# Two batches of a selective-scan layer as one unrolled pipeline over 64 heads

## The chip, the core and the metric

The kernel runs on one core of a Trainium2 chip. Five engines work beside each other and meet by semaphores: PE (TensorE, matmuls), DVE (VectorE), ACT (ScalarE), POOL (GpSimd) and SP (SyncE), which here only issues DMAs. The metric is the device time in microseconds, the median of several executions. Lower is better.

## The reference, cut to what matters

Two layers follow each other, each an attention-like part and a feed-forward part. The change touches the first part of layer 0 alone, a selective scan over 512 tokens, 2 batches and 32 heads of 128 channels:

```python
proj = x @ in_proj_w.T
gate, hbc, dt = jnp.split(proj, [I, I + CD], axis=-1)
conv = causal depthwise convolution of hbc, 4 taps
hbc = jax.nn.silu(conv + conv_b)
hs, B, C = jnp.split(hbc, [I, I + G * N], axis=-1)   # G = 8 groups, N = 128
B = jnp.tile(B, (1, 1, H // G, 1)); C = jnp.tile(C, (1, 1, H // G, 1))   # head h uses group h % 8
...
Y_diag = jnp.einsum('bclhn,bcshn,bhcls,bcshd->bclhd', Cc, Bc, Lmat, Xc)
Y_off = jnp.einsum('bclhn,bchdn,bhcl->bclhd', Cc, states_prev, state_decay)
y = (Y_diag + Y_off).reshape(b, s, H, P) + D_res
h32 = y * jax.nn.silu(gate)
g = h32.reshape(b, s, I // gs, gs)                   # gs = 512: four heads share one root
h32 = (g * jax.lax.rsqrt(var + EPS)).reshape(b, s, I)
return norm_w * h32 @ out_proj_w.T
```

## The kernel before

**Groups.** For each batch, B and C of eight groups are made first: 12 bf16 matmuls (`group_rows`, L450), ACT's first tap (L873), six taps on DVE (L1281), two tanh (L883), DVE's products `BT` and `CT` (L1288, L1291), four fp32 matmuls C x B and four transposes (L479, L482), two copies to `CB` and `Btok` (L887, L889) and POOL's mask (L1859). All eight stay in SBUF while the batch's heads run.

**Scan.** `scan_slot` on each engine writes one slot: head n is at stage 0, head n-1 at stage 1, head n-2 at stage 2. `slots` writes 8 slots, a hardware loop of three rounds of 8, and 7 more to drain; then batch 1 starts with its groups. PE in a slot: projection of `x` into bank 0 (`px`, L450), turning `xT` of head n-1 (L506), states of head n-2 into bank 5 (L515), the broadcast of `cs` of head n (the running sum of the decay) into bank 3 from three bf16 pieces `csT` (L527), a tile of the output product (L589, four heads' rows, into bank 6 or 7), the diagonal product of head n-1 into bank 5 (L538), once in four slots the sums of squares (L570), the chunk products into bank 4 (L551), the projection of the gate into bank 1 (`pg`, L450).

DVE in a slot: `Mm` (L1319), `gs` (L1325), tap 1 (L1333), `yv` (L1364, it empties bank 5), taps 2 and 3, three states (L1348, L1351) with the sum of an output tile (L1396) among them, and `xT` (L1381). One slot in four has ten of the root's twelve small steps (`root_step`, L1410 to L1426, 128x4) between these. ACT: tanh of the gate (L905), first tap (L910), `Xdt` (L919), exp `Em` (L927), the high half of the next weights `whl` (L932), `rel` (L937), square (L949), exp into bank 3 (L954), tanh into bank 2 (L959). POOL: `Xw` (L1812), `yb` (L1824), the low half of the weights (L1830), `CE` (L1835), the norm's factor on `wB` (L1841), the sum of squares (L1850).

Every engine works in the order written. The waits that set the pace: PE's turn waits for `xT`; PE's diagonal product waits for `Mm`, `Xdt` and for `yv` of the head before (`yc_done`), since both heads use bank 5; `yb` waits for `yv`, the square for `yb`, and the exp and the tanh that `xT` needs stand behind the square on ACT. In batch 1 the groups wait until batch 0 has left the buffers that they share with it. SP loads weights of 256 KB (`wA`) and 128 KB (`wB`) a head.

## Time and profile before

| | us |
|---|---|
| median of 3 runs | 1213.24 (1211.51 to 1215.61) |
| the profiled execution | 1214.29 |
| its span, first to last instruction | 1212.5 |
| PE busy | 958.9 (79%) |
| DVE busy | 899.9 (74%) |
| ACT busy | 657.0 (54%) |
| POOL busy | 520.6 (43%) |

The profile is of one execution; times in its rows are from the span's start. PE's matmuls overlap, so the distance between starts says more than one's duration. The granted clock is the share of full speed (2.4 GHz) that PE was given. A row of the timeline joins equal instructions that follow each other: start, duration of all, engine, line, operation, tiles, count, and in brackets the idle time before and who ended it.

### The profile page before, as it was taken

What the parts mean: (1) busy time and instruction counts of PE and PEld (TensorE: products, weight loads), DVE (VectorE), ACT (ScalarE), POOL (GpSimd) and SP (SyncE); (2) the same over time, 40 slices, a digit from 0 to 9 for tenths busy, and PEclk for the clock granted to TensorE, in tenths of its full rate; (3) what the DMA queues carried; (4) which work ended last, traced back from release to release, by engine and by line L of the source; (5) the groups of instructions that cost most, each with busy time, mean ns of one, the idle gap of its engine ahead of it and who ended that gap; (6) DMA issues with size and microseconds to landing.
All of it is one profiled execution on the core that took longest, in us unless ns stands there. A gap on an engine that the chain in (4) does not pass through costs nothing. (4 is left out here: it accounts for less than half of the span.)

```text
span 1212.5 us, 19613 instructions
## 1 busy us (share of the span) xinstructions
PE 958.9 (79%) x5524; PEld 645.3 (53%) x5524; DVE 899.9 (74%) x1667; ACT 657.0 (54%) x1421; POOL 520.6 (43%) x497
## 2 busy tenths in 40 slices
...
DMA packets 25353, 43.24 MB, mean 36 GB/s; under 512 B 3218, under 2 KB 15250, under 8 KB 24466
## 3 DMA queue, kind: packets, MB, share of 16 engines
...
HBM read 40.60 MB, written 1.05 MB: 34 GB/s over the span
## 5 line engine op out<-in xcount | busy, mean ns | idle before, releaser
L450 PE MATMUL bank<-hTs,whl 128*128 128x512 bf16 x768 | 177.7, 380 | 3.7 <-DVE u L1333 3.7
L1333 DVE SCALAR_TENSOR_TENSOR u<-bank,chn,u 128x511 f32<-128x511 f32 (+2 forms) x192 | 143.0, 745 | 29.2 <-ACT u L910 23.3
L589 PE MATMUL bank<-wB,yb 128*128 128x256 f32 x512 | 137.8, 418 | 3.9 <-DVE acc L1396 2.7
L1812 POOL TENSOR_TENSOR xbuf<-xbuf,dec 128x384 f32<-128x384 f32 x64 | 53.2, 832 | 172.6 <-ACT xbuf L919 172.6
L589 PEld LDWEIGHTS bank<-wB,yb 128*128 128x128 f32 x512 | 108.8, 214 | 22.8 <-DVE rg L1426 3.4
L450 PEld LDWEIGHTS bank<-hTs,whl 128*128 128x128 bf16 x768 | 75.4, 98 | 81.2 <-POOL whl L1830 6.4
L1878 POOL TENSOR_TENSOR hfs<-hf,hfs 128x512 bf16<-128x512 f32 x44 | 50.8, 1156 | 119.9 <-ACT hfs L1030 119.9
L450 PE MATMUL bank<-hTs,w13s 128*128 128x512 bf16 x372 | 94.7, 403 | 3.5 <-DVE hf L1536 1.9
L919 ACT ACTIVATE xbuf<-bank,dtv 128x128 f32<-128x128 f32 x256 | 72.5, 370 | 33.7 <-PE bank L506 33.7
L1824 POOL TENSOR_TENSOR yb<-yv,gs 128x512 f32<-128x512 f32 x64 | 81.3, 1271 | 6.7 <-DVE yv L1364 6.6
L1868 POOL TENSOR_TENSOR w13s<-w,w13s 128x256 bf16<-128x256 f32 (+1 forms) x22 | 23.2, 1090 | 135.4 <-ACT w13s L994 135.4
L753 PE MATMUL bank<-Ex,VW 128*80 128x512 f32 x128 | 72.8, 658 | 10.8 <-ACT Ex L1111 10.0
L538 PE MATMUL bank<-Mm,xbuf 128*128 128x128 f32 x512 | 68.8, 277 | 10.9 <-DVE yv L1364 8.9
L1103 ACT ACTIVATE aw<-bank,scl 128x512 f32<-128x512 f32 x64 | 43.4, 684 | 62.7 <-PE bank L740 37.1
L910 ACT ACTIVATE u<-bank,chn 128x512 f32<-128x512 f32 x64 | 49.7, 777 | 50.9 <-PE bank L450 50.9
L538 PEld LDWEIGHTS bank<-Mm,xbuf 128*128 128x128 f32 x512 | 66.1, 193 | 19.0 <-ACT xbuf L919 14.4
L1830 POOL TENSOR_TENSOR whl<-wA,whl 128x512 bf16<-128x512 f32 x64 | 74.2, 1160 | 2.0 <-ACT whl L932 1.9
L659 PE MATMUL bank<-w2s,hfs 128*128 128x256 bf16 x528 | 68.8, 283 | 7.9 <-POOL hfs L1878 7.9
L937 ACT ACTIVATE rel<-bank,cs 128x128 f32<-128x128 f32 x256 | 74.6, 406 | 0.0
L1281 DVE SCALAR_TENSOR_TENSOR gs<-bank,bcp,gs 128x511 f32<-128x511 f32 (+2 forms) x96 | 64.3, 739 | 6.0 <-ACT gs L873 5.9
L506 PE MATMUL bank<-cst,xT 128*128 128x128 f32 x256 | 41.0, 283 | 34.8 <-DVE xT L1381 34.8
L1348 DVE COPY xbuf<-bank 128x128 f32<-128x128 f32 x64 | 18.5, 288 | 67.1 <-PE bank L551 67.1
...
## 6 DMA issues: line engine op xcount, KB each, us to landing
wA<-in_win SPq DMA_DIRECT2D x65, 256.0 KB, 2.6
...
```

The source lines that it names most:

```text
L450: last = nc.tensor.matmul(out, wpart(a, kt), hpart(c, kt), start=n == 0, stop=n == 5)
L538: nc.tensor.matmul(bank[5][:, c * P:(c + 1) * P], Xdt[:, j % 2, c * P:(c + 1) * P], Mm[:, j % 2, c * P:(c + 1) * P], start=c == 0, stop=c ...
L589: last = nc.tensor.matmul(bank[6 + t % 2][:, 0:D], yb[:, y0 + m, t * P:(t + 1) * P], wB[:, y0 + m, :], start=m == 0, stop=m == HG - 1)
L659: last = nc.tensor.matmul(bank[6 + t // 2][:, (t % 2) * D:(t % 2 + 1) * D], hfs[:, a, m % 3, t * P:(t + 1) * P], w2s[:, c, f, :], start=Fa ...
L753: nc.tensor.matmul(bank[VB[par]][0:OC, :], VW[:, par, i * OC:(i + 1) * OC], Ex[:, i, :], start=i == 0, stop=i == 3).then_inc(q["a_PV"], 1)
L919: last = nc.scalar.activation(Xdt[:, j % 2, t * P:(t + 1) * P], bank[2][:, t * P:(t + 1) * P], ACT.Copy, scale=dtv[:, b * TB + t, bass.ds( ...
L937: last = nc.scalar.activation(rel[:, t * P:(t + 1) * P], bank[3][:, t * P:(t + 1) * P], ACT.Relu, scale=-1.0, bias=cs[:, b * TB + t, bass. ...
L1281: nc.vector.scalar_tensor_tensor(out=o, in0=bank[GB[par] + m][:, 0:S - d], scalar=w(m, 3 - d), in1=o, op0=ALU.mult, op1=ALU.add)\
L1333: nc.vector.scalar_tensor_tensor(out=u[:, i % 2, d:S], in0=bank[0][:, 0:S - d], scalar=chn[:, bass.ds(hcol, 1), 3 - d:4 - d].squeeze(1), i ...
L1812: nc.gpsimd.tensor_tensor(Xw[:, j % 2, :].rearrange("p (t n) -> p t n", n=P), Xdt[:, j % 2, 0:S - P].rearrange("p (t n) -> p t n", n=P), d ...
L1824: nc.gpsimd.tensor_tensor(yb[:, j, :], yv[:, j % 2, :], gs[:, j % 4, :], ALU.mult)\
L1830: nc.gpsimd.tensor_tensor(whl[:, nx, 1, :], wA[:, nx, :], whl[:, nx, 0, :], ALU.subtract).then_inc(q["wsplit"], 1)
```

## The change

One pipeline runs over all 64 heads, written out without a loop: 70 slots. The heads of a batch come in another order (`ORDER`): the 16 heads of groups 0 to 3 first, then the 16 of groups 4 to 7. Groups are numbered 0 to 15 over both batches. The first four are made ahead of the scan as before. The other 12 are made in slots 0 to 47, a quarter in each slot, all through bank 7: r0 (slot number divisible by 4) projects B and takes its taps, r1 makes `BT` and projects C with its taps, r2 turns `BT` and makes `CT`, r3 makes the product C x B. The output tiles have bank 6 alone. The sums of squares stand right behind the projection of `x`, and the root runs in that slot (r2), its last three steps behind `xT`; the sum of the tile stands behind `xT`, then follows the group's work.

The broadcast of `cs` comes from memory: once written to DRAM (`csd`), it is loaded for each head into all partitions (`csb`, 256 KB). The high half of the weights isn't copied: PE reads the upper 16 bits of each fp32 weight in place (`wAh`), and `wA` has four buffers. `wB` is loaded for four heads at once.

```diff
+N = B * H
+FIRST = 4
+ORDER = [HG * k + m for k in list(range(0, NG, 2)) + list(range(1, NG, 2)) for m in range(HG)]
...
-        wA = sb("wA", [P, 2, 512])
-        whl = sb("whl", [P, 2, 2, 512], bf16)
-        wB = sb("wB", [P, 8, D])
+        ug = sb("ug", [P, 2, S])
+        wA = sb("wA", [P, 4, 512])
+        wAh = wA[:, :, :].bitcast(bf16).rearrange("p a (n c) -> p a n c", c=2)[:, :, :, 1]
+        wAl = sb("wAl", [P, 2, 512], bf16)
+        wB = sb("wB", [P, 2, HG, D])
...
+        def head(n):
+
+            return (n, n // H, ORDER[n % H]) if 0 <= n < N else None
+
+        def out_tile(s):
+
+            m = s - 6
+            return (m % TB, m // TB) if 0 <= m < N else None
+
+        def former(gq):
+
+            b, g = gq // G, gq % G
+            return H * (b - 1) + ORDER.index(H - G + g) + 1 if b else 0
...
+                if h0 := head(s):
+                    n, b, hid = h0
+                    if n > 1:
+                        sp.wait_ge(q["rel_done"], n - 1)
+                    sp.dma_start(csb[:, n % 2, :], csd[b, hid].partition_broadcast(P)).then_inc(d_cb[n % 2], 16)
+                    if n > 3:
+                        sp.wait_ge(q["pg"], n - 3)
+                    sp.dma_start(wA[:, n % 4, :], io["win"][hid]).then_inc(d_wA[n % 4], 16)
...
+            def group_slot(s):
+
+                gq, r = FIRST + s // 4, s % 4
+                if gq >= B * G:
+                    return
+                if r == 0:
+                    pe.wait_ge(q["c_evac"], 2 * gq)
+                    if s == 0:
+                        pe.wait_ge(q["csr_done"], 1)
+                    group_half(gq, 0, bank[7][:, :]).then_inc(q["c_proj"], 1)
+                if r == 1:
+                    pe.wait_ge(q["c_step"], 6 * gq + 3)
+                    group_half(gq, 1, bank[7][:, :]).then_inc(q["c_proj"], 1)
+                if r == 2:
+                    pe.wait_ge(q["c_step"], 6 * gq + 6)
+                    pe.wait_ge(q["c_bc"], 2 * gq + 1)
+                    turn_keys(bank[7])
+                if r == 3:
+                    pe.wait_ge(q["c_evac"], 2 * gq + 1)
+                    pe.wait_ge(q["c_bc"], 2 * gq + 2)
+                    meet(gq, bank[7])
...
+                if e and e[0] == 0:
+                    k = e[1]
+                    if s - 1 < N:
+                        pe.wait_ge(q["rc_step"], 3 * (s - 1))
+                    pe.wait_ge(q["sq_add"], 3 * (k + 1))
...
+                    if TB * k + t:
+                        pe.wait_ge(q["oa_done"], TB * k + t)
+                    for m in range(HG):
+                        last = nc.tensor.matmul(bank[6][:, 0:D], yb[:, HG * (k % 2) + m, t * P:(t + 1) * P],
+                                                wB[:, k % 2, m, :], start=m == 0, stop=m == HG - 1)
...
+            def group_slot(s):
+
+                gq, r = FIRST + s // 4, s % 4
+                if gq >= B * G:
+                    return
+                if r == 0:
+                    act.wait_ge(q["c_bc"], 2 * gq - 3)
+                    act.wait_ge(q["c_proj"], 2 * gq + 1)
+                    group_taps(gq, 0, bank[7][:, :])
+                if r == 1:
+                    act.wait_ge(q["c_step"], 6 * gq + 3)
+                    group_tanh(gq, 0)
+                    act.wait_ge(q["c_bc"], 2 * gq - 2)
+                    act.wait_ge(q["c_proj"], 2 * gq + 2)
+                    group_taps(gq, 1, bank[7][:, :])
+                if r == 2:
+                    act.wait_ge(q["c_step"], 6 * gq + 6)
+                    group_tanh(gq, 1)
+                    keep_keys(gq, bank[7][:, :])
+                if r == 3:
+                    keep_meet(gq, bank[7][:, :])
...
+                nc.vector.scalar_tensor_tensor(out=BT[:], in0=thx[:, 0, :], scalar=1.0, in1=ub(gq, 0),
+                                               op0=ALU.add, op1=ALU.mult).then_inc(q["c_bc"], 1)
...
+            def group_slot(s):
+
+                gq, r = FIRST + s // 4, s % 4
+                if gq >= B * G or r == 3:
+                    return
+                if r == 1:
+                    keys(gq)
+                if r == 2:
+                    queries(gq)
+                    return
+                dve.wait_ge(q["c_raw"], 2 * gq + r + 1)
+                for d in (1, 2, 3):
+                    if d > 1:
+                        dve.wait_ge(q["c_step"], 6 * gq + 3 * r + d - 1)
+                    group_tap(gq, r, d, bank[7])
...
+                root(7, 8)
...
+                root(9, 10, 11)
...
+                group_slot(s)
...
+            for gq in range(FIRST):
+                first_group(gq)
+            clamp_gates(0)
+            for s in range(N + 6):
+                scan_slot(s)
```

The products, taps, roots and sizes are the same otherwise, and so is everything behind the scan.

**DVE, from `xT` of a head to `yv` of the next slot.** Before, in the loop:

```order
L1381 SCALAR_TENSOR_TENSOR xT<-bank,u 128x512
L1302 REGISTER_ALU
L1319 TENSOR_TENSOR Mm<-CB,bank 128x512
L1325 SCALAR_TENSOR_TENSOR gs<-thg,bank 128x512
L1332 REGISTER_ALU
L1333 ISA
L1333 SCALAR_TENSOR_TENSOR u<-bank,chn,u 128x511
L1364 ISA
L1364 SCALAR_TENSOR_TENSOR yv<-xT,chn,bank 128x512
```

After, in the first r1 slot that has an output tile (`ug` is the group's tile of taps, `L1401` makes `xT`, `L1382` `yv`):

```order
L1401 SCALAR_TENSOR_TENSOR xT<-bank,u 128x512
L1412 SCALAR_TENSOR_TENSOR acc<-bank,rg,acc 128x256
L1281 SCALAR_TENSOR_TENSOR BT<-thx,ug 128x512
L1273 SCALAR_TENSOR_TENSOR ug<-bank,bcp,ug 128x511
L1273 SCALAR_TENSOR_TENSOR ug<-bank,bcp,ug 128x510
L1273 SCALAR_TENSOR_TENSOR ug<-bank,bcp,ug 128x509
L1341 TENSOR_TENSOR Mm<-CB,bank 128x512
L1345 SCALAR_TENSOR_TENSOR gs<-thg,bank 128x512
L1424 TENSOR_SCALAR ssv<-bank 128x4
L1354 SCALAR_TENSOR_TENSOR u<-bank,chn,u 128x511
L1427 TENSOR_SCALAR nwt<-ssv 128x4
L1382 SCALAR_TENSOR_TENSOR yv<-xT,chn,bank 128x512
```

Between `xT` and `Mm` four instructions of the group now stand, and two steps of the root ahead of `yv`.

**PE, from the diagonal product to the turning of `xT`, in the slot with the sums.** Before:

```order
L589 MATMUL bank<-wB,yb 128x256 x4
L538 MATMUL bank<-Mm,xbuf 128x128 x4
L568 REGISTER_ALU
L570 MATMUL bank<-cst,sqa 128x1 x4
L551 MATMUL bank<-xbuf,Btok 128x128 x3
L450 MATMUL bank<-hTs,whl 128x512 x6
L496 REGISTER_ALU
L492 REGISTER_ALU
L450 MATMUL bank<-hTs,whl 128x512 x6
```

After, at the end of an r1 slot (`L563` the diagonal product, `L572` the chunk products, `L520` the sums):

```order
L563 MATMUL bank<-Mm,xbuf 128x128 x4
L572 MATMUL bank<-xbuf,Btok 128x128 x3
L438 MATMUL bank<-hTs,wbs 128x512 x6
L438 MATMUL bank<-hTs,wA 128x512 x4
L438 MATMUL bank<-hTs,wAl 128x512 x2
L438 MATMUL bank<-hTs,wA 128x512 x4
L438 MATMUL bank<-hTs,wAl 128x512 x2
L520 MATMUL bank<-cst,sqa 128x1 x4
L531 MATMUL bank<-cst,xT 128x128 x4
```

The sums moved from ahead of the chunk products to behind the next head's projection, and half a group's projection (`wbs`) stands ahead of the gate's.

## Rows read from the trace of the kernel before

**Rows 1.** Timeline: `xT` of five heads, and the step behind the scan.

```profile
107.13 0.69 DVE L1381 SCALAR_TENSOR_TENSOR xT<-bank,u 128x512 f32<-128x512 f32 x1 [0.77 <-ACT bank L959]
...
167.13 0.68 DVE L1381 SCALAR_TENSOR_TENSOR xT<-bank,u 128x512 f32<-128x512 f32 x1
...
360.65 0.69 DVE L1381 SCALAR_TENSOR_TENSOR xT<-bank,u 128x512 f32<-128x512 f32 x1
...
441.92 0.69 DVE L1381 SCALAR_TENSOR_TENSOR xT<-bank,u 128x512 f32<-128x512 f32 x1 [0.83 <-ACT bank L959]
...
697.37 0.69 DVE L1381 SCALAR_TENSOR_TENSOR xT<-bank,u 128x512 f32<-128x512 f32 x1
...
720.10 2.49 DVE L1446 TENSOR_TENSOR acc<-acc,gm 128x1024 f32<-128x1024 f32 x2
```

**Rows 2.** Timeline: taps of groups 3 and 7, three taps of one head.

```profile
70.55 4.02 DVE L1281 SCALAR_TENSOR_TENSOR gs<-bank,bcp,gs 128x511 f32<-128x511 f32 x6
...
92.32 4.02 DVE L1281 SCALAR_TENSOR_TENSOR gs<-bank,bcp,gs 128x511 f32<-128x511 f32 x6
...
104.05 2.31 DVE L1333 SCALAR_TENSOR_TENSOR u<-bank,chn,u 128x511 f32<-128x511 f32 x3 [5.84 <-ACT u L910]
```

**Rows 3.** Timeline: PE in one plain slot.

```profile
202.07 0.60 PE L506 MATMUL bank<-cst,xT 128*128 128x128 f32 x4
...
203.17 0.38 PE L527 MATMUL bank<-csT,identb 96*128 96x512 bf16 x1
...
203.39 1.89 PE L589 MATMUL bank<-wB,yb 128*128 128x256 f32 x8
...
205.12 1.05 PE L538 MATMUL bank<-Mm,xbuf 128*128 128x128 f32 x8
...
206.68 2.75 PE L450 MATMUL bank<-hTs,whl 128*128 128x512 bf16 x12
...
209.27 0.65 PE L506 MATMUL bank<-cst,xT 128*128 128x128 f32 x4
```

**Rows 4.** Timeline: DVE and ACT around the same slot.

```profile
201.10 0.68 DVE L1381 SCALAR_TENSOR_TENSOR xT<-bank,u 128x512 f32<-128x512 f32 x1
...
204.09 0.74 DVE L1364 SCALAR_TENSOR_TENSOR yv<-xT,chn,bank 128x512 f32<-128x512 f32 x1
...
207.74 0.58 ACT L959 ACTIVATE bank<-u 128x512 f32<-128x512 f32 x1
...
208.51 0.69 DVE L1381 SCALAR_TENSOR_TENSOR xT<-bank,u 128x512 f32<-128x512 f32 x1
```

**Rows 5.** Timeline: slot with the root, and PE in the next.

```profile
219.51 0.74 DVE L1364 SCALAR_TENSOR_TENSOR yv<-xT,chn,bank 128x512 f32<-128x512 f32 x1
...
223.00 1.00 POOL L1835 TENSOR_TENSOR xbuf<-CT,Em 128x384 f32<-128x384 f32 x1
...
223.10 0.92 DVE L1423 SCALAR_TENSOR_TENSOR nwt<-nwt,ssv 128x4 f32<-128x4 f32 x1
...
226.34 0.69 DVE L1381 SCALAR_TENSOR_TENSOR xT<-bank,u 128x512 f32<-128x512 f32 x1
...
227.16 0.65 PE L506 MATMUL bank<-cst,xT 128*128 128x128 f32 x4 [2.38 <-DVE xT L1381]
...
228.57 3.54 PE L589 MATMUL bank<-wB,yb 128*128 128x256 f32 x8
```

**Rows 6.** The page: weight loads, and the load of weights with us to landing.

```profile
L450 PEld LDWEIGHTS bank<-hTs,whl 128*128 128x128 bf16 x768 | 75.4, 98 | 81.2 <-POOL whl L1830 6.4
...
L538 PEld LDWEIGHTS bank<-Mm,xbuf 128*128 128x128 f32 x512 | 66.1, 193 | 19.0 <-ACT xbuf L919 14.4
...
wA<-in_win SPq DMA_DIRECT2D x65, 256.0 KB, 2.6
```

**Rows 7.** Windows: stretch, length, busy PE PEld DVE ACT POOL, granted clock, DMA share, GB/s.

```profile
101.00:360.00 259.00, 235.65 (x1420) 175.86 (x1418) 211.00 (x417) 189.54 (x476) 174.52 (x178) 0.96 0.17 49
227.70:232.70 5.00, 5.00 (x24) 4.21 (x23) 3.63 (x6) 4.26 (x13) 3.35 (x4) 0.66 0.00 0
```

More of the change, by code:

```diff
@@ L88, in build_block @@
         etot = sb("etot", [P, NT, H])
-        csp = sb("csp", [P, NT, PIECES, H], bf16)
-        csT = sb("csT", [PIECES * H, T], bf16)
+        csb = sb("csb", [P, 2, S])
+        csd = nc.dram_tensor("csd", (B, H, S), fp32, kind="Internal").ap()
         wbs = sb("wbs", [P, 2, G, 512], bf16)
@@ L473, in group_products @@
-            def group_products(g, b):
-                pe.wait_ge(q["c_bc"], 2 * (G * b + g) + 2)
-                if not (type(g) is int and G * b + g == 0):
-                    pe.wait_ge(q["c_evac"], G * b + g)
-                for t in range(TB):
-                    last = nc.tensor.matmul(bank[2][:, t * P:(t + 1) * P], BT[:, t * P:(t + 1) * P],
-                                            CT[:, bass.ds(g, 1), t * P:(t + 1) * P].squeeze(1), start=True, stop=True)
-                for t in range(TB):
-                    last = nc.tensor.transpose(bank[3][:, t * P:(t + 1) * P], BT[:, t * P:(t + 1) * P], ident)
-                last.then_inc(q["c_mm"], 1)
@@ new lines, in turn_keys, with meet @@
+            def turn_keys(out):
+                for t in range(TB):
+                    last = nc.tensor.transpose(out[:, t * P:(t + 1) * P], BT[:, t * P:(t + 1) * P], ident)
+                last.then_inc(q["c_mm"], 1)
+            def meet(gq, out):
+                for t in range(TB):
+                    last = nc.tensor.matmul(out[:, t * P:(t + 1) * P], BT[:, t * P:(t + 1) * P],
+                                            CT[:, gq % G, t * P:(t + 1) * P], start=True, stop=True)
+                last.then_inc(q["c_mm"], 1)
@@ L531, in scan_slot @@
-                out_slot(i, it, b)
-                if h1:
-                    j = h1[0]
-                    pe.wait_ge(q["xdt_done"], n1 + 1)
-                    pe.wait_ge(q["M_done"], n1 + 1)
-                    since("yc_done", n1)
-                    for c in range(TB):
-                        nc.tensor.matmul(bank[5][:, c * P:(c + 1) * P], Xdt[:, j % 2, c * P:(c + 1) * P],
-                                         Mm[:, j % 2, c * P:(c + 1) * P], start=c == 0, stop=c == 0,
-                                         skip_group_check=True)
@@ L542, in scan_slot @@
-                if h1:
-                    since("rc_step", 3 * n1)
-                if (e := out_event(i, it, 7)) and e[0] == 0:
-                    pe.wait_ge(q["rg_step"], ROOT * (NG * b + e[2]) + 1)
-                sums_slot(i, it, b)
-                if h1:
-                    j = h1[0]
-                    pe.wait_ge(q["xw_done"], n1 + 1)
-                    for c in range(TB - 1):
-                        last = nc.tensor.matmul(bank[4][:, c * P:(c + 1) * P], Btok[:, j, c, :],
-                                                Xw[:, j % 2, c * P:(c + 1) * P], start=True, stop=True)
-                    last.then_inc(q["ps"], 1)
@@ new lines, in scan_slot @@
+                if h1:
+                    n = h1[0]
+                    pe.wait_ge(q["xdt_done"], n + 1)
+                    pe.wait_ge(q["M_done"], n + 1)
+                    if n:
+                        pe.wait_ge(q["yc_done"], n)
+                    else:
+                        pe.wait_ge(q["c_step"], 6 * FIRST)
+                    for c in range(TB):
+                        nc.tensor.matmul(bank[5][:, c * P:(c + 1) * P], Xdt[:, n % 2, c * P:(c + 1) * P],
+                                         Mm[:, n % 2, c * P:(c + 1) * P], start=c == 0, stop=c == 0,
+                                         skip_group_check=True)
+                    if n:
+                        pe.wait_ge(q["rc_step"], 3 * n)
+                    if e and e[0] == 0:
+                        pe.wait_ge(q["rg_step"], ROOT * e[1] + 1)
+                    pe.wait_ge(q["xw_done"], n + 1)
+                    for c in range(TB - 1):
+                        last = nc.tensor.matmul(bank[4][:, c * P:(c + 1) * P], Btok[:, h1[2] % G, c, :],
+                                                Xw[:, n % 2, c * P:(c + 1) * P], start=True, stop=True)
+                    last.then_inc(q["ps"], 1)
@@ L981, in _ @@
+            first_rows(1)
+            first_tanh(0)
+            for gq in range(1, FIRST):
+                if gq + 1 < FIRST:
+                    first_rows(gq + 1)
+                first_tanh(gq)
+                first_evac(gq - 1)
+            first_evac(FIRST - 1)
+            for s in range(N + 2):
+                scan_slot(s)
             if stop == 0:
```

706 lines of the change are left out of this document (296 added, 410 removed).

## Prediction

> **What bounds the kernel now.** I read the timeline of the scan first, by one instruction per head: DVE's product that makes `xT`, from whose start to the next I count a slot. The first starts at 107.13, that of the ninth head at 167.13, the last of batch 0 at 360.65, the first of batch 1 at 441.92, the last of all at 697.37, and the step behind the scan at 720.10 [rows 1]. So the seam between the batches takes 81.3 us where a slot takes 8 or 9, and eight groups of B/C ahead of either batch take their own time: the taps of group 3 start at 70.55, those of group 7 at 92.32, 5.44 us a group [rows 2].
>
> In the steady scan four slots make a period (four heads share one root): 167.13 to 201.10, 34.0 us [rows 1, 4]. In a plain slot PE has no gap: from turning `xT` at 202.07 to the next at 209.27 is 7.2 us, filled by states, the broadcast of `cs` (0.22), the out tile (1.73), the diagonal and chunk products (1.56) and two projections (2.59) [rows 3]. But a loop through the other engines is as long: `yv` ends at 204.83, POOL's `yb`, ACT's square, exp and tanh follow, and `xT` starts at 208.51 [rows 4]; then PE turns it. And PE may start the diagonal product of the next head only when `yv` has emptied bank 5: `yv` ends 2.76 into the slot, the product starts at 3.05 [rows 3, 4]. That 0.3 us is all the slack DVE has. In the slot with the root it is used up: `xT` comes at 226.34, PE has stood for 2.38 us, and its clock falls: the tile that took 1.89 now takes 3.54, granted clock 0.66 over 5 us [rows 5, 7]. At half clock (1.2 GHz) one such stretch costs PE about 1.65 us.
>
> **The change, part by part.** I start from the profiled execution's 1214.3 us (span 1212.5, 1.8 around it), which stands 1.05 above the median of the runs.
>
> *Seam and front, removed.* Four groups stay ahead: first `xT` at 107.1 - 4 x 5.44 = 85.3. The seam becomes a slot among others. With no price for the groups inside, 64 heads would need 60.0 for the first eight slots [rows 1] and 34.0 for each period after.
>
> *Broadcast of `cs` by matmul, removed.* 0.22 us of PE a slot; ACT loses the copy of the weights' high half too, but waits anyway. A plain period: 34.0 - 4 x 0.22 = 33.1. In its place come 64 loads of 256 KB. Such a load lands in 2.6 us [rows 6]; each is issued some one and a half slots before its exp and the weights a slot before POOL splits them, so I cost both at 0; exposed whole, it would be 2.6 us a slot.
>
> *Weights read as every second bf16.* LDWEIGHTS of packed bf16 takes 98 ns, of fp32 193 [rows 6]; a projection's matmul has 2.59/12 = 0.216 us. Between these ends it is hidden: 0.
>
> *12 groups inside.* PE per group: 12 matmuls (2.6), 4 turns and 4 products of two steps each (12 steps, by the 14 steps that take 1.56 [rows 3], 1.4), 4.0 us a period. ACT, POOL have room. DVE gets, after `xT` and the tile's sum and **ahead of** `Mm`, `gs`, the first tap and `yv`: three taps in slot r0, `BT` and three taps in r1, `CT` in r2, nothing in r3. Three taps on one tile depend on each other and take 2.31 [rows 2]. Here DVE's 0.3 us of slack decides. One period by hand, 0 at PE's turn in r0, durations as in [rows 3, 4]:
> - r0: PE 7.2 - 0.22 + 1.3 = 8.3 long. `xT` ends at 7.1; sum and taps until 9.75; `Mm`, `gs`, tap, `yv` (2.65) until 12.4, that is 4.1 into r1.
> - r1: PE's diagonal waits until 4.2, 1.3 more than before; then 1.56 + 1.3 (group) + 2.6 + 0.9 (sums, 8 such steps, now ahead of the turn): 10.5, so r2 starts at 18.8. DVE: `yv` 12.4, the loop's 3.2 and `xT` to 16.3, sum 16.7.
> - `BT` reads two SBUF tiles. The root's steps with such operands end only with POOL's instruction: POOL 223.00 for 1.00, DVE's 128x4 step 223.10 for 0.92 [rows 5]. POOL is then busy until 5.2 behind `yv`, 17.6. I take the wait (0.9; without one 0), as that row is the nearest: `BT` to 18.3, taps 20.6, `Mm` to `yv` with two root steps 23.5, 4.7 into r2.
> - r2: `yv` to the end of `xT` was 220.25 to 227.03, 6.8 [rows 5]; three root steps move behind `xT` and POOL has an addition less in this slot: 5.9 (up to 6.8). `xT` ends 29.4, r3 starts 29.5.
> - r3: three root steps, sum, `CT`, then to `yv`: 33.8, 4.3 in; PE's 1.56 + 0.95 + 2.6 behind it: 9.5.
> Together 39.0 us against 34.0: the groups cost 5.9 a period over 33.1, though PE has only 4.0 of work more, because PE waits for `yv` in three slots of four. The ends: if all waits hide, PE's 4.0 fills its 2.4 us gap first, 33.1 + 4.0 - 2.4 = 34.7; if the root slot keeps its 6.8 and two more low-clock stretches fall where PE is late, 39.0 + 0.9 + 3.3 = 43.2.
>
> On that wait the Trainium skill, "SBUF — State Buffer", section "SBUF: two separate sides", says that a DVE instruction with two SBUF inputs and a GpSimd one that reads SBUF exclude each other for the whole instruction. By it the 512-column `BT` waits as the 128x4 steps do, giving 39.0; were only such small steps caught, the period would be 38.1 and the sum 10 us less. The rows of the root agree; no row before shows a large product beside POOL.
>
> *Sums.* First `xT` 85.3. First eight slots 60.0 + 10.8 (5.4 for each of two periods) = 70.8. Ten periods at 39.0 = 390. Last fifteen slots, without groups, 4 x 33.1 - 7.4 = 125.0. Last `xT`: 671.1. The tail was 22.7 [rows 1]; with one bank for the tiles instead of two its last tiles alternate with their sums, about 0.85 us three times: 25.3. End 696.4 instead of 720.1: **-23.7**. Behind it nothing changes. 1214.3 - 23.7 - 1.05 = 1189.5, say **1190 us**. Each us of the period is worth 11 us, so the break-even is a period of 41.2.
>
> **Rivals.**
> *A, PE remains the bound.* DVE catches up in r3 and the groups hide in gaps: period 34.7, 1190 - 11 x 4.3 = 1143. For it: DVE is busy 211 us of 259 in the scan [rows 7], and it stands idle ahead of the first state. Against it: that idle time lies behind `yv`, the inserted taps ahead of it.
> *B, slower: low clock.* In the old period one gap of 2.4 us brought one low stretch. The new one has four gaps of 1.3 to 1.8 (three for `yv`, one for `xT`). If each brings one, three more, each 1.65 on PE's path, the period is 44.0: 1190 + 55 = 1245; with two, 1226. It decides from 1.3 paid stretches on. Against it: where PE waits for `yv` anyway, a low stretch costs nothing, since DVE's time doesn't depend on it (r1, r3).
> *C, loads in the way.* SP's queue is in order: `csb` waits for `rel_done`, behind it stand the weights and the out weights. If one landing is exposed in each slot: 64 x 2.6 = 166, 1356. Against it: every load has a slot and more.
> *D, the seam stays*, since head 32 or group 8 waits for buffers of batch 0. In the reordered heads `former()` asks for heads 13 to 16 when group 8 to 11 is made in slots 16 to 31, so nothing stands. If it stood once, it would cost what the seam holds besides a slot and eight groups, 81.3 - 8.5 - 43.5 = 29: 1219.
>
> **How the numbers follow.** My case, period 37 to 41: 1168 to 1212, chance 0.58. A 0.17, B 0.19, C 0.03, D 0.03. The range must reach into A and B: 1148 to 1224. A measurement tells some 0.3% (3.6 us) from no change. Faster: A, D in part, and nearly all of my case: 0.74. Same 0.05. Slower: B, C and the edge: 0.21.
>
> **What would show it.** `xT` of heads 0, 8, 48, 63 near 85, 156, 546, 671, and the step behind the scan near 696. In the period: PE's idle time ahead of the diagonal product put down to `yv`, 1.3 to 2 us in slots r1 to r3 and none in r0; `BT` at over 1 us where `CT` is near 0.7; slots of 8.3, 10.5, 10.7, 9.5. A: no wait for `yv`, PE full. B: granted clock in the scan under 0.9 where it was 0.96 [rows 7]. C: ACT's `Em` waits for a DMA. I am wrong above all if DVE's chain through `Mm` to `yv` gets shorter or longer than I laid it, a us a period being 11 us, or if the clock falls more often.

## The result, and the profile after

| | before | after |
|---|---|---|
| median, us | 1212.39 (1211.51 to 1215.61) | 1164.83 (1160.94 to 1166.34) |
| ratio, 95% interval | | 0.9599 (0.9576 to 0.9622) |
| profiled execution, its span | 1214.3, 1212.5 | 1164.2, 1162.4 |
| PE, DVE busy | 958.9, 899.9 | 920.3, 900.9 |

The kernel is 47.6 us faster, twice the forecast 22 to 24. The timeline of the product that makes `xT` (now L1401; heads 0, 8, 48, 63) and of the step behind the scan (L1455) answers to [rows 1]:

```profile
87.42 0.69 DVE L1401 SCALAR_TENSOR_TENSOR xT<-bank,u 128x512 f32<-128x512 f32 x1 [0.67 <-ACT bank L969]
...
158.19 0.69 DVE L1401 SCALAR_TENSOR_TENSOR xT<-bank,u 128x512 f32<-128x512 f32 x1 [0.38 <-ACT bank L969]
...
529.15 0.69 DVE L1401 SCALAR_TENSOR_TENSOR xT<-bank,u 128x512 f32<-128x512 f32 x1 [0.39 <-ACT bank L969]
...
649.03 0.69 DVE L1401 SCALAR_TENSOR_TENSOR xT<-bank,u 128x512 f32<-128x512 f32 x1 [0.17 <-ACT bank L969]
...
673.03 2.48 DVE L1455 TENSOR_TENSOR acc<-acc,gm 128x1024 f32<-128x1024 f32 x2
```

The ten periods between heads 8 and 48 take 371.0 us, 37.1 each; without groups a period is 31.8 (heads 48 to 60). The step behind the scan comes 47.1 us earlier. (In all profiles of this study, 489.3 to 492.4 us lie behind that step.) One execution of a_bt_behind below, 1422.6 us at a granted clock of 0.64, was a slow one and is left out of its time.

PE in one period with groups. Turns (L531) start at 226.16 (r0), 234.44 (r1), 244.55 (r2) and 253.91 (r3), so the slots take 8.28, 10.11 and 9.36, and the last the other 9.3:

```profile
221.04 1.13 PE L563 MATMUL bank<-Mm,xbuf 128*128 128x128 f32 x8 [1.13 <-DVE yv L1382]
...
228.99 1.05 PE L563 MATMUL bank<-Mm,xbuf 128*128 128x128 f32 x8
...
238.22 1.13 PE L563 MATMUL bank<-Mm,xbuf 128*128 128x128 f32 x8 [0.79 <-DVE yv L1382]
...
244.55 0.63 PE L531 MATMUL bank<-cst,xT 128*128 128x128 f32 x4
...
248.85 1.13 PE L563 MATMUL bank<-Mm,xbuf 128*128 128x128 f32 x8 [1.26 <-DVE yv L1382]
...
253.91 0.66 PE L531 MATMUL bank<-cst,xT 128*128 128x128 f32 x4 [0.24 <-DVE xT L1401]
```

PE waits for `yv` in r3, r1 and r2 and not in r0. The gap of 2.38 ahead of the turn behind the root [rows 5] is 0.24. Without groups that gap is 0.68, and a plain slot takes 561.75 - 554.76 = 6.99, where it was 7.2 [rows 3]:

```profile
538.21 1.02 PE L520 MATMUL bank<-cst,sqa 128*128 128x1 f32 x8 [0.93 <-POOL sqa L1858]
...
546.95 0.66 PE L531 MATMUL bank<-cst,xT 128*128 128x128 f32 x4 [0.68 <-DVE xT L1401]
...
554.76 0.60 PE L531 MATMUL bank<-cst,xT 128*128 128x128 f32 x4
...
561.75 0.60 PE L531 MATMUL bank<-cst,xT 128*128 128x128 f32 x4
```

DVE in slots r1 and r2 (`BT` is L1281, the root's steps are L1424 to L1440). POOL's instructions in the fence behind it are `yb` (L1835), the low half of the weights (L1842), `CE` (L1846), the factor on `wB` (L1852) and the sum of squares `sqa` (L1858).

```profile
242.35 1.48 DVE L1281 SCALAR_TENSOR_TENSOR BT<-thx,ug 128x512 f32<-128x512 f32 x1
...
247.96 0.74 DVE L1382 SCALAR_TENSOR_TENSOR yv<-xT,chn,bank 128x512 f32<-128x512 f32 x1
...
249.35 0.81 DVE L1435 TENSOR_TENSOR nwt<-rg 128x4 f32<-128x4 f32 x1
...
250.74 0.42 DVE L1437 SCALAR_TENSOR_TENSOR nwt<-nwt,ssv 128x4 f32<-128x4 f32 x1
...
251.29 0.83 DVE L1440 SCALAR_TENSOR_TENSOR rg<-nwt,rg 128x4 f32<-128x4 f32 x1
...
252.30 0.39 DVE L1435 TENSOR_TENSOR nwt<-rg 128x4 f32<-128x4 f32 x1
...
253.17 0.69 DVE L1401 SCALAR_TENSOR_TENSOR xT<-bank,u 128x512 f32<-128x512 f32 x1
```

And POOL's rows of the same stretch:

```profile
242.01 1.26 POOL L1858 TENSOR_TENSOR sqa<-sqa,ysq 128x512 f32<-128x512 f32 x1
...
248.87 1.27 POOL L1835 TENSOR_TENSOR yb<-yv,gs 128x512 f32<-128x512 f32 x1 [1.45 <-DVE yv L1382]
250.10 1.04 POOL L1842 TENSOR_TENSOR wAl<-wA 128x512 bf16<-128x512 f32 x1
251.10 1.00 POOL L1846 TENSOR_TENSOR xbuf<-CT,Em 128x384 f32<-128x384 f32 x1
252.07 0.60 POOL L1852 TENSOR_TENSOR wB<-wB,chn 128x256 f32<-128x256 f32 x1
```

`BT` started at 242.35 beside `sqa`, which ended at 243.27, and took 1.48. The four slow root steps end at 250.16, 251.16, 252.12 and 252.69; POOL's four instructions end at 250.14, 251.14, 252.10 and 252.67.

Windows of the kernel after (stretch, length, busy PE PEld DVE ACT POOL, granted clock, DMA share, GB/s). Full speed was granted from 107 to 677 us, where the kernel before had a half-speed stretch in nearly every period [rows 7]; DVE now works 0.90 of the time (172.89 of 193):

```profile
530.00:640.00 110.00, 102.01 (x633) 77.21 (x643) 94.19 (x193) 78.21 (x195) 76.77 (x80) 1.00 0.28 82
167.00:360.00 193.00, 173.63 (x1059) 127.82 (x1077) 172.89 (x335) 135.70 (x324) 120.14 (x124) 1.00 0.23 73
```

### The profile page after: what moved, and what is told of

It reads as the page before. It is cut to its first block and busy times, and to the rows that moved or that the text cites. A ratio compares the mean times of both kernels' runs of the same rounds, so it can differ in the third digit from the quotient of the medians.

```text
span 1162.4 us, 16855 instructions
## 1 busy us (share of the span) xinstructions
PE 920.3 (79%) x5377; PEld 615.5 (53%) x5454; DVE 900.9 (78%) x1663; ACT 633.3 (54%) x1356; POOL 512.5 (44%) x496
## 5 line engine op out<-in xcount | busy, mean ns | idle before, releaser
L438 PE MATMUL bank<-hTs,wA 128*128 128x512 bf16 x456 | 121.2, 383 | 3.7 <-DVE u L1354 0.8
L551 PE MATMUL bank<-wB,yb 128*128 128x256 f32 x512 | 121.5, 380 | 2.5 <-DVE acc L1412 2.5
L563 PE MATMUL bank<-Mm,xbuf 128*128 128x128 f32 x512 | 71.7, 284 | 45.3 <-DVE yv L1382 43.0
L1835 POOL TENSOR_TENSOR yb<-yv,gs 128x512 f32<-128x512 f32 x64 | 81.5, 1274 | 42.7 <-DVE yv L1382 42.4
L551 PEld LDWEIGHTS bank<-wB,yb 128*128 128x128 f32 x512 | 92.4, 190 | 13.6 <-DVE acc L1412 3.7
L563 PEld LDWEIGHTS bank<-Mm,xbuf 128*128 128x128 f32 x512 | 64.3, 193 | 61.4 <-issue 54.8
L438 PE MATMUL bank<-hTs,w13s 128*128 128x512 bf16 x354 | 90.1, 402 | 4.8 <-DVE hf L1545 1.9
L947 ACT ACTIVATE rel<-csb,cs 128x128 f32<-128x128 f32 x256 | 82.2, 413 | 0.0
L438 PEld LDWEIGHTS bank<-hTs,wA 128*128 128x128 bf16 x512 | 50.5, 99 | 53.1 <-issue 2.6
L438 PE MATMUL bank<-hTs,wAl 128*128 128x512 bf16 x255 | 76.2, 380 | 0.2 <-issue 0.2
L1273 DVE SCALAR_TENSOR_TENSOR ug<-bank,bcp,ug 128x511 f32<-128x511 f32 (+2 forms) x84 | 61.7, 744 | 8.1 <-ACT ug L845 6.4
L1034 ACT ACTIVATE hfs<-hf 128x512 bf16<-128x512 f32 x44 | 27.7, 629 | 73.9 <-DVEq L1548 45.1
L955 ACT ACTIVATE ysq<-yb 128x512 f32<-128x512 f32 x48 | 30.3, 630 | 66.5 <-POOL yb L1835 66.5
```

Of the source, the lines that this page charges most:

```text
L438: last = nc.tensor.matmul(out, wpart(a, kt), hpart(c, kt), start=n == 0, stop=n == 5)
L551: last = nc.tensor.matmul(bank[6][:, 0:D], yb[:, HG * (k % 2) + m, t * P:(t + 1) * P], wB[:, k % 2, m, :], start=m == 0, stop=m == HG - 1)
L563: nc.tensor.matmul(bank[5][:, c * P:(c + 1) * P], Xdt[:, n % 2, c * P:(c + 1) * P], Mm[:, n % 2, c * P:(c + 1) * P], start=c == 0, stop=c ...
L947: last = nc.scalar.activation(rel[:, t * P:(t + 1) * P], csb[:, n % 2, t * P:(t + 1) * P], ACT.Relu, scale=-1.0, bias=cs[:, b * TB + t, hi ...
L1273: nc.vector.scalar_tensor_tensor(out=o, in0=pa[:, 0:S - d], scalar=bcp[:, gq % G, m, 3 - d:4 - d], in1=o, op0=ALU.mult, op1=ALU.add).then_ ...
L1835: nc.gpsimd.tensor_tensor(yb[:, n % 8, :], yv[:, n % 2, :], gs[:, n % 4, :], ALU.mult)\
```

## The experiments

Each edit is of the kernel after, if not said otherwise. "Period" is read from the starts of `xT`: heads 8 to 48 (with groups) and 48 to 60 (without). A time without a ratio is that of a single execution (before and after apart); there the periods carry the reading. They repeat within 0.1 us, but for a period in which a lone half-speed stretch falls.

| kernel | us | period with groups | without |
|---|---|---|---|
| before | 1212.4 | | 34.0 |
| after | 1164.8 | 37.1 | 31.8 |
| b_root_behind (before, edited) | 1189.2, ratio to before 0.9804 (0.9784 to 0.9825) | | 32.0 |
| a_root_ahead | 1162.6, 0.9569 (0.9550 to 0.9589) | 37.0 | 31.8 |
| a_late2 | 1184.5 | 38.6 | 33.5 |
| a_late4 | 1220.9 | 40.3 | 36.1 |
| a_narrow_taps | 1139.0 | 34.6 | 31.8 |
| a_one_matmul | 1168.7 | 37.1 | 31.8 |
| a_first8 | 1167.7, 0.9621 (0.9600 to 0.9642) | 37.1 (8 of them) | 31.8 |
| b_rb_narrow_cs (before, edited) | 1189.8 | | 31.9 (32.4 with one period of 33.4 that has a lone half-speed stretch) |
| a_pe_more | 1168.1 | 37.3 | 32.1 |
| a_act_more | 1162.9 | 37.1 | 31.8 |
| a_bt_behind | 1161.9, 0.9593 (0.9562 to 0.9623) | 36.5 | 31.8 |
| a_square_last | 1159.3, 0.9578 (0.9545 to 0.9611) | 36.8 | 31.7 |
| a_yv_first | 1142.3, 0.9420 (0.9401 to 0.9440) | 35.0 | 31.9 |
| a_yv_sq | 1140.5, 0.9414 (0.9387 to 0.9441) | 34.9 | 31.9 |
| a_yv_swap | 1140.9, 0.9422 (0.9399 to 0.9445) | 34.9 | 31.9 |

### The root's steps and the low clock

**b_root_behind.** In the kernel before, three steps move behind `xT`:

```diff
-                    rms_link(8 + c)
+                    if c == 0:
+                        rms_link(8)
...
                 state(2)
-                rms_link(11)
                 rms_link(0)
...
                 rms_link(1)
+                for k in (9, 10, 11):
+                    rms_link(k)
```

> The kernel before, with one edit: the last three of the root's small steps stand behind xT instead of ahead of it. Theory 1: the gap of 2.38 us ahead of PE's turn brings the low-clock stretch. xT of the root slot comes about 1.2 us earlier (one step of 1.04 and two of 0.17 leave the path), the gap shrinks to about 1.2, the low-clock stretch (1.65 us of PE) goes too, and the period falls from 34.0 to 31.1: 15 periods, 1212 - 43 = 1169 us, no low-clock stretch in the scan. Rival: the low clock has another cause, such as the broadcast of cs or the loop; the stretch stays and only the gap shrinks: period 32.8, 1194 us. Third: another wait fills the gap, 34.0 and 1212.

Measured: period 32.0, 23.7 us less at the step behind the scan. The gain is clear of no change, but its interval reaches down to 1.75%. PE's timeline there:

```profile
221.73 0.65 PE L506 MATMUL bank<-cst,xT 128*128 128x128 f32 x4 [1.31 <-DVE xT L1381]
...
223.70 0.39 PE L527 MATMUL bank<-csT,identb 96*128 96x512 bf16 x1 [0.65 <-DVE Mm L1319]
```

The gap fell from 2.38 to 1.31 and the regular low clock went with it: granted clock 1.00 over 495 to 670 us, 0.94 over the same stretch in the kernel before. (One lone stretch fell in batch 0, from about 254.6, behind a gap of 1.23; that period took 33.5.) A new wait of 0.65 for `Mm` took some back, since `Mm` stands behind the moved steps: 34.0 - 1.07 - 1.65 + 0.65 = 31.9. So theory 1 held for the clock and missed the new wait. In the kernel before, these few lines are worth half of what the whole change brought.

**a_root_ahead** is the opposite edit of the kernel after:

```diff
-                root(7, 8)
+                root(7, 8, 9, 10, 11)
...
-                root(9, 10, 11)
```

> The kernel after, with one edit: the last three steps of the root stand ahead of xT again. Theory 1 (gaps near 1.3 us bring no low clock in this scan): xT of the root slot 0.6 to 0.9 later, PE's gap ahead of the turn about 1 us instead of 0.24 (1.5 instead of 0.68 without groups), no low-clock stretch, part of it made good since the three steps no longer stand ahead of the next yv: period 37.1 + 0.4, 1165 + 6 = 1171 us. Rival: each such gap brings a low-clock stretch as in the kernel before: 1.65 more a period, 1165 + 16 x 2 = 1197 us, mean granted clock in the scan near 0.96.

PE's timeline, the turn behind the root and the next diagonal product with groups, and the turn without:

```profile
255.80 0.66 PE L531 MATMUL bank<-cst,xT 128*128 128x128 f32 x4 [0.82 <-DVE xT L1401]
...
259.39 1.13 PE L563 MATMUL bank<-Mm,xbuf 128*128 128x128 f32 x8 [0.54 <-DVE yv L1382]
...
548.35 0.66 PE L531 MATMUL bank<-cst,xT 128*128 128x128 f32 x4 [1.27 <-DVE xT L1401]
```

The gap ahead of the turn became 0.82, the next wait for `yv` 0.54 instead of 1.13, and the period stayed, where theory 1 had 0.4 more. Without groups the gap became 1.27 and the wait for `yv` of 0.53 went, and that period stayed too. The steps cost the same on either side of `xT`, since they stand between one `yv` and the next either way. Its time isn't told from that of the kernel after. No low clock came at 0.8 or 1.3.

So the same move that gave 2.0 a period in the kernel before gives nothing in the kernel after. There POOL's addition no longer stands in the root's slot, and the first of the three steps, which had taken 1.04 beside it, takes 0.16 (the kernel before, then a_root_ahead):

```profile
224.77 1.04 DVE L1421 TENSOR_TENSOR nwt<-rg 128x4 f32<-128x4 f32 x1
...
254.55 0.16 DVE L1434 TENSOR_TENSOR nwt<-rg 128x4 f32<-128x4 f32 x1
```

To end the regular low clock either was enough: the steps moved in the kernel before, or the other edits of the kernel after with the steps still ahead of `xT`.

**a_late2, a_late4** hold the turn back once a period (a_late4 with 4 in place of 2):

```diff
+                    if e and e[0] == 0:
+                        for m in range(2):
+                            dve.wait_ge(q["dm"], 2 * e[1] + m)
+                            nc.vector.scalar_tensor_tensor(out=xT[:, n % 4, :], in0=bank[2][:, :], scalar=1.0,
+                                                           in1=u[:, n % 2, :], op0=ALU.add, op1=ALU.mult)\
+                                .then_inc(q["dm"], 1)
+                        dve.wait_ge(q["dm"], 2 * (e[1] + 1))
```

> The kernel after, with the product that makes xT done three times instead of once in the slot with the root (same operands, same tile), which holds PE's turn back by about 2 x 0.6 = 1.2 us once a period. PE's gap ahead of that turn: 0.24 + 1.2 = 1.4 us with groups, 0.68 + 1.2 = 1.9 without. Theory: gaps of this size brought no regular low clock in the kernels so far (1.31 in the kernel before with its root steps moved, 1.26 in the kernel after); the period grows by 1.2, 38.3 and 33.0, and 16 x 1.2 = 19 us: 1184, no regular low-clock stretch. Rival: from 1.4 on each gap brings one: without groups 33.0 + 1.65 = 34.6.

> As the kernel with three such products, but five of them: 2.4 us later than in the kernel after. PE's gap ahead of the turn: 2.6 us with groups, 3.1 without, at or above the 2.38 of the kernel before. Theory 1: the low-clock stretch is back in each period. Without groups PE pays it: 31.8 + 2.4 + 1.65 = 35.8; with groups part of it hides behind the wait for yv (1.13 in r3): 37.1 + 2.4 + 0.5 = 40.0; 1165 + 12 x 2.9 + 4 x 4.0 = 1216 us. Rival: the low clock of the kernel before had nothing to do with the gap's length: 34.2 and 39.5, 1165 + 16 x 2.4 = 1203 us and no stretch.

Each extra product held the turn back by 0.75 us (the gap went from 0.24 to 1.76 and 3.21). PE's timeline of a_late2, the turn behind the root with groups and four times without:

```profile
253.99 0.66 PE L531 MATMUL bank<-cst,xT 128*128 128x128 f32 x4 [1.76 <-DVE xT L1408]
...
558.92 0.66 PE L531 MATMUL bank<-cst,xT 128*128 128x128 f32 x4 [2.19 <-DVE xT L1408]
592.17 0.66 PE L531 MATMUL bank<-cst,xT 128*128 128x128 f32 x4 [2.20 <-DVE xT L1408]
625.57 0.93 PE L531 MATMUL bank<-cst,xT 128*128 128x128 f32 x4 [2.20 <-DVE xT L1408]
659.71 0.92 PE L531 MATMUL bank<-cst,xT 128*128 128x128 f32 x4 [2.19 <-DVE xT L1408]
```

And of a_late4, once with and once without groups:

```profile
268.73 0.88 PE L531 MATMUL bank<-cst,xT 128*128 128x128 f32 x4 [3.21 <-DVE xT L1408]
269.40 1.49 PE L539 MATMUL bank<-xbuf 128*128 128x128 f32 x6
...
587.77 1.11 PE L531 MATMUL bank<-cst,xT 128*128 128x128 f32 x4 [3.64 <-DVE xT L1408]
...
589.96 3.54 PE L551 MATMUL bank<-wB,yb 128*128 128x256 f32 x8
```

With a gap of 1.76 in each period with groups no low clock came, nor with the 2.07 of the first. Of the four gaps of 2.2 the last two brought it (there the turn takes 0.92 for 0.66), the first two didn't. With 3.2 to 3.6 it came behind 8 of 11 gaps with groups and behind each without, as these windows of a_late4 show:

```profile
165.00:520.00 355.00, 302.57 (x1792) 225.51 (x1826) 317.36 (x603) 228.80 (x544) 204.45 (x210) 0.97 0.22 66
570.00:700.00 130.00, 111.15 (x641) 85.26 (x650) 109.27 (x220) 80.63 (x201) 77.72 (x82) 0.92 0.22 70
```

Where groups run, a stretch mostly costs nothing or 0.3 (periods of 40.0 or 40.3), since PE waits for `yv` in r3 anyway; two that lasted about twice as long cost 1.4 and 1.5 (periods of 41.4 and 41.5). Where no groups run, PE pays it: 36.1 - 31.8 = 4.3, of which 4 x 0.75 = 3.0 is the delay and 1.3 the clock. So in these kernels gaps of up to 1.8 brought no regular low clock and gaps of 3.2 and more brought it most times. In between, equal gaps of 2.2 went either way, and the 2.1 to 2.4 of the kernel before brought a stretch nearly each time. A few lone stretches came behind shorter gaps (in a_yv_first one behind a wait of 1.03). So the length of the gap matters, but does not settle it alone; what else goes into it stays open.

### What a group costs inside the scan

**a_narrow_taps** and **a_one_matmul** take DVE's and PE's share of the groups away in turn:

```diff
-                o = ub(gq, m)[:, d:S]
-                nc.vector.scalar_tensor_tensor(out=o, in0=pa[:, 0:S - d], scalar=bcp[:, gq % G, m, 3 - d:4 - d],
+                w = S - d if gq < FIRST else 16
+                o = ub(gq, m)[:, d:d + w]
+                nc.vector.scalar_tensor_tensor(out=o, in0=pa[:, 0:w], scalar=bcp[:, gq % G, m, 3 - d:4 - d],
```
```diff
+                if gq >= FIRST:
+                    return nc.tensor.matmul(out, wbs[:, 0, g, m * KT * P:(m * KT + 1) * P],
+                                            hTs[:, 0, 0, b * S:(b + 1) * S], start=True, stop=True)
```

> The kernel after, but for the 12 groups inside the scan DVE's six taps and BT work on 16 columns instead of about 512, so that B and C of these groups are left incomplete; all waits, and all work of PE, ACT and POOL, stay. It takes about 4.9 us of DVE out of a period. Theory: what DVE does ahead of yv sets the period; the waits of slots r1 (0.79) and r2 (1.26) vanish, PE's work (28.0 of four plain slots, 0.87 sums, 4.0 of the group) and the wait of r3 (1.1 for CT and the root's steps) stay: 34.6 us a period, 12 x 2.5 = 30 us less, 1135. Rival (PE's added work is the price, and the waits are only where it shows): the period stays over 36.5, 1158 or more.

> The kernel after, but for the 12 groups inside PE's half projections take one matmul instead of six, so that B and C of these groups are left incomplete; DVE's, ACT's and POOL's work stays. It takes 2 x 5 x 0.216 = 2.2 us of PE out of a period. Theory: in r1, r2 and r3 PE waits for yv and the loop of DVE, POOL and ACT sets the pace; only r0, where PE doesn't wait, gets shorter, by 0.7 to 1.1: period 36.0 to 36.4, 12 x 0.9 = 11 us less, 1154. Rival (PE is the bound): period 34.9, 1139.

a_narrow_taps: 34.6 against 37.1. With DVE's work gone, the waits for `yv` in r1 and r2 are gone, as the theory had it to the tenth. a_one_matmul: taking 2.2 us of PE's work out gained nothing, where 0.7 to 1.1 was expected. Slot r0 did get shorter, from 8.28 to 7.21, but PE then waits longer for `yv` instead (its timeline in a_one_matmul, r1 and r2):

```profile
240.68 1.13 PE L566 MATMUL bank<-Mm,xbuf 128*128 128x128 f32 x8 [1.86 <-DVE yv L1385]
...
251.31 1.13 PE L566 MATMUL bank<-Mm,xbuf 128*128 128x128 f32 x8 [1.50 <-DVE yv L1385]
```

So DVE's work between two `yv` sets the period, and these 2.2 of the 4.0 us that a group adds to PE are free beside it.

**a_first8** makes eight groups ahead and eight in slots 16 to 47:

```diff
-FIRST = 4
+FIRST = 8
...
-                gq, r = FIRST + s // 4, s % 4
-                if gq >= B * G:
+                gq, r = FIRST + (s - 16) // 4, s % 4
+                if s < 16 or gq >= B * G:
```

> The kernel after, with eight groups ahead of the scan and the other eight in slots 16 to 47. Theory: a group inside costs 37.1 - 31.8 = 5.3 us a period, a group ahead 5.44, so four groups moved from inside to ahead change nothing: first xT 87.4 + 21.8 = 109.2, last xT and the time as the kernel after within 3 us, 1162 to 1168. Rival (a group inside fills gaps and costs 1.6, as the forecast's rival A had it): 4 x 3.8 = 15 us slower, 1180.

1167.7, 2.9 above the kernel after, inside the expected band: a group inside costs 37.1 - 31.8 = 5.3, one ahead 5.44 [rows 2]. (The first `xT` came at 111.95, where 109.2 was expected.) Moving groups inside by itself gains nothing as DVE's order stands; what is left to pay is that the two batches then follow without a seam, which no run took by itself.

### The small terms

**b_rb_narrow_cs, a_pe_more, a_act_more**: the broadcast made narrow in b_root_behind; a matmul of the same size, and an exp of ACT, done twice in the kernel after.

```diff
-                        bank[3][:, :], identb96[:, bass.ds(hcol, 1)].to_broadcast([PIECES * H, P]),
-                        csT[:, b * S:(b + 1) * S], start=True, stop=True, skip_group_check=True)\
+                        bank[3][:, 0:16], identb96[:, bass.ds(hcol, 1)].to_broadcast([PIECES * H, P]),
+                        csT[:, b * S:b * S + 16], start=True, stop=True, skip_group_check=True)\
```
```diff
+                if twice:
+                    nc.tensor.matmul(out, wpart(0, 0), hpart(0, 0), start=True, stop=True)
```
```diff
+                    nc.scalar.activation(Em[:, n % 2, :], csb[:, n % 2, P:S], ACT.Exp).then_inc(q["dm"], 1)
+                    act.wait_ge(q["dm"], n + 1)
```

> The kernel before with its last three root steps behind xT, and the matmul that broadcasts cs done for 16 of 512 columns, so that the decay of the other columns is wrong; it prices that matmul. Theory (PE has no gap in a plain slot): 4 x 0.2 = 0.8 us a period, 32.0 to 31.2, and 15 x 0.8 + 1 = 13 us of 1189: 1176. Rival: DVE, ACT and POOL are as long in the plain slots (0.3 us of slack): at most half of it, 31.6, 1182.

> The kernel after, with the first of the six matmuls of the projection of x done twice (same result): 0.216 us more of PE in each slot, about what the broadcast of cs took before. Theory (in the kernel after PE has no slack in a plain slot): without groups 4 x 0.216 = 0.86 a period, 31.8 to 32.7; with groups only r0 pays, 37.1 to 37.3; 1165 + 3.7 x 0.86 + 12 x 0.2 = 1171 us. Rival (the 0.22 hides, as it did in the kernel before with the narrow broadcast): 31.9, 37.1, 1165.

> The kernel after, with ACT's exp of 384 columns (Em) done twice: 0.42 to 0.5 us more of ACT a slot, about what the copy of the weights' high half took before. Theory (ACT waits 0.7 us for yb behind it in each plain slot): nothing, periods 31.8 and 37.1, 1165. Rival (that copy, and not the broadcast matmul, is what the plain slot lost, 7.2 to 7.0): 32.6 without groups, 1169 or more.

The narrow broadcast gained about 0.1 a period, less than either theory. PE's timeline: the broadcast (L527) starts at 201.56 and the tile at 201.59, 0.03 later where it was 0.22 [rows 3], but the tile's matmuls then take 0.08 more, and the turns stay 7.19 apart:

```profile
201.56 0.17 PE L527 MATMUL bank<-csT,identb 96*128 96x16 bf16 x1
201.59 1.97 PE L589 MATMUL bank<-wB,yb 128*128 128x256 f32 x8
203.40 1.09 PE L538 MATMUL bank<-Mm,xbuf 128*128 128x128 f32 x8
...
207.65 0.66 PE L506 MATMUL bank<-cst,xT 128*128 128x128 f32 x4
```

The loop through DVE, POOL and ACT was as long as PE there. In the kernel after, 0.216 us more of PE costs 0.35 a period without groups and 0.2 with, not 4 x 0.216: only the two plain slots pay. More work on ACT costs nothing. So the broadcast was worth 0.1 to 0.35 a period, not 0.88. Which of the edits brought the plain slot from 7.2 to 6.99 was not isolated.

### Moves towards a faster kernel

**a_bt_behind**: `keys(gq)` (it makes `BT`) behind the three taps of r1. **a_square_last**: ACT's square behind exp and tanh.

> The kernel after, with BT behind the three taps of slot r1 instead of ahead of them, where POOL's sum of squares is over. Theory: BT takes 0.68 instead of 1.48, yv of slot r2 ends 0.8 earlier, PE's wait there falls from 1.26 to 0.5, and the period from 37.1 to 36.3: 12 periods, 1165 - 9.6 = 1155 us. Rival: xT of the root slot waits for the root's steps anyway or the saved time turns up as another wait: within 3 us of 1165.

> The kernel after, with ACT's exp and tanh ahead of the square of yb, so that xT no longer stands behind yv, yb and the square. Theory of the forecast (this loop is as long as PE's slot, and is what limits in r1 to r3 once yv is late): xT comes 0.3 us earlier in slots r0, r1 and r3, the next yv with it, and PE waits less: period 37.1 - 0.6 to 0.9, 1156 us. Rival: DVE's own order (yv, taps, states, xT) is as long as the loop and the sums of squares, now 1.1 us later, hold PE: no gain or slower, 1165 to 1178.

```profile
238.41 0.68 DVE L1281 SCALAR_TENSOR_TENSOR BT<-thx,ug 128x512 f32<-128x512 f32 x1
```

`BT` took 0.68 at its new place, PE's wait in r2 went from 1.26 to 0.66, and the period from 37.1 to 36.5; on the whole time, whose interval is 0.3% either way, this isn't told from noise. The square's move gave 0.3 a period, half of the least that the theory asked for.

**a_yv_first** puts four pieces of DVE's work behind `yv`:

```diff
-                if r == 1:
-                    keys(gq)
                 if r == 2:
-                    queries(gq)
                     return
...
-                for d in (1, 2, 3):
+                for d in (1, 2) if r == 0 else (1, 2, 3):
...
+                if r == 1:
+                    keys(gq)
...
+                if s % 4 == 1 and FIRST + s // 4 < B * G:
+                    dve.wait_ge(q["c_step"], 6 * (FIRST + s // 4) + 2)
+                    group_tap(FIRST + s // 4, 0, 3, bank[7])
+                if s % 4 == 3 and FIRST + s // 4 < B * G:
+                    queries(FIRST + s // 4)
                 root(2)
...
                 tap(3)
+                add_tile(e and e[0])
...
+                add_tile(e and e[0] == 0)
```

> The kernel after with four moves of DVE's work to behind yv, nothing else: the sum of output tiles 1 to 3 behind the third tap, CT behind yv in slot r3, the third tap of B behind yv in slot r1, BT behind the taps of slot r1. Theory: PE's waits for yv lose 0.6 in r3, 0.8 (all) in r1 and 1.0 in r2: period 37.1 - 2.4 = 34.7, without groups 31.5; 1165 - 29 - 1 = 1135 us. Rival: the work put behind yv delays xT, since DVE's idle time there is 0.8 us a slot: PE then waits for xT instead and the period falls by no more than BT's 0.6: 1157 us.

> The kernel after with both sets of moves: DVE's group work and sums behind yv where there is room, and ACT's square behind exp and tanh. The square's move took 0.34 a period from the kernel after, the other 2.05. Theory: DVE is busy without a gap from r1 to r3, so earlier exp and tanh help only in r0 and r3, where xT still waits 0.38 and 0.16 for ACT: period 35.05 to 34.8, 1139 us. Rival: the sums of squares come 1.1 us later and hold PE: no gain, 1142 to 1150.

> The kernel with DVE's group work behind yv, and ACT's first tap of C ahead of the tanh of B in slot r1, since DVE now takes the taps first and waits 0.46 for that tap. Theory (DVE is busy without a gap from there to r3, so each of its waits counts): period 35.05 to 34.6, 1137 us. Rival: the root slot's steps and xT take up the time, 35.0 and 1142.

a_yv_first: period 35.0 (34.7 expected) and 31.9 without groups (31.5 expected), 1142.3 us (1135 expected): a further 22.5 us, or 1.9%, below the kernel after. PE's waits in r2 and r3 are 0.85 and 0.52, that of r1 is gone:

```profile
241.37 1.13 PE L563 MATMUL bank<-Mm,xbuf 128*128 128x128 f32 x8 [0.85 <-DVE yv L1395]
...
250.01 1.13 PE L563 MATMUL bank<-Mm,xbuf 128*128 128x128 f32 x8 [0.52 <-DVE yv L1395]
```

The square's move (a_yv_sq) brings 0.15 more a period. DVE's wait of 0.46 for ACT's first tap goes with a_yv_swap, but the period falls by 0.2 only. On the whole time the three kernels can't be told apart; each beats both given kernels.

## Why the prediction was right in direction and half the size

| step | forecast | measured |
|---|---|---|
| first `xT` | 85.3 | 87.4 (83.7 to 89.1 over the profiles with four groups ahead) |
| first eight slots | 70.8 | 70.8 |
| ten periods with groups | 390 (39.0) | 371.0 (37.1) |
| last fifteen slots | 125.0 | 119.9 |
| tail | 25.3 | 24.0 (24.0 to 27.8 over the profiles of edits of the kernel after) |
| step behind the scan | 696.4 | 673.0 |

**Right.** The seam went, and four groups stay ahead at their price. DVE's chain from one `yv` to the next decides, and PE waits for it in r1, r2 and r3 and not in r0, by 0.79, 1.26 and 1.13 where 1.3 to 2 was forecast. a_narrow_taps against a_one_matmul shows that this is the cause. `BT` was held up as the Trainium skill ("SBUF — State Buffer", "SBUF: two separate sides") has it for a DVE instruction with two SBUF inputs beside a GpSimd one that reads SBUF: 1.48 here, 0.68 in a_bt_behind. The loads stayed hidden: no `Em` waits for a DMA. The tail fell into the alternation of tile and sum that was forecast. That the first eight slots took just the 70.8 forecast is luck: without groups they take 58.5 (a_first8) where the sum had 60.0, and two groups in them cost 12.3 where it had 10.8.

**Wrong, 19.0 us: the period of 39.0.** The hand sum was 1.9 too long, and the slots show where: r0 8.28 for 8.3, r1 10.11 for 10.5, r2 9.36 for 10.7, r3 9.3 for 9.5. Most is the root slot. The step "three root steps move behind `xT` and POOL has an addition less: 5.9" is mis-sized: from the end of `yv` (248.70) to that of `xT` (253.86) it is 5.2, 1.6 less than the 6.8 of the kernel before, where 0.9 was put down. In the kernel before, five steps each ended with one of POOL's five instructions, the last, the addition L1850, at 225.79; in the kernel after there are four instructions and four such steps. Either edit alone frees the fifth step: b_root_behind, with the addition still there and the steps moved, takes from 215.88 to 221.59, 5.7; a_root_ahead, without the addition and with the steps ahead, takes from 250.00 to 255.74, also 5.7. So the first edit of the two gives 1.1 and the second another 0.5 or 0.6. How much of the 1.1 is the fifth step wasn't split: POOL also starts `yb` 0.2 sooner behind `yv` in a_root_ahead than in the kernel before. The rest is that `yv` ends 3.6 into r1 and 4.15 into r2, where 4.1 and 4.7 were laid out. An estimate of why: DVE's products last 0.68 and start 0.60 apart (`BT`, taps and `Mm` of a_bt_behind start at 236.18, 238.41 and 239.01), and at each join of two groups of rows the sum kept 0.08.

**Wrong, 5.1 us: the period of 33.1 without groups.** It measured 31.8. The step took the 34.0 of the kernel before with its gap of 2.38 and its low clock, and took off the broadcast. The working moved the root's steps and POOL's addition in the periods with groups and forgot them here. b_root_behind shows what the gap and the low clock were worth: 2.0 a period net. In the kernel after the gap is 0.68, and with the steps ahead of `xT` again (a_root_ahead) it is 1.27 at the same 31.8. The broadcast's 0.88 was wrong the other way, by 0.5 or more.

**Rival B, slower through low clock,** counted gaps and not their length. Gaps of up to 1.3 brought no low stretch in the kernel after (only lone ones in its edits), and the one of 2.38 that had brought them was gone. No case of the forecast had the low clock getting less. **Rival A** (a group costs only 1.6) is ruled out by 5.3. **C and D** did not occur: no `Em` waits for a DMA, and from the last `xT` of batch 0 (372.41) to the first of batch 1 (380.52) it is 8.1.

Of the 47.6 us, then, what b_root_behind also reaches is 23 to 24. The other half is the difference, which was not split by a run. An estimate from the profiles of b_root_behind, a_first8 and the kernel after: 19.8 for the shorter front and 70.8 for the seam, less 66.0 for the 12 groups inside and 1.2 for the longer tail, 23.4.
